# Two attention phases of a transformer kernel: norm, projections and score maxima one batch earlier in a software pipeline

## Chip, cores and metric

One core of a Trainium2 chip runs the whole program. The metric is device time in microseconds from the program's start to its end: the median of three runs is 3821.44 us before the change (3792.84, 3821.44, 3825.76).

## What is computed

Four transformer layers over 16 batches of 256 tokens with 128 channels. Each layer adds a gated attention and a gated feed-forward part to the residual `x`. The change touches the attention of layer 0 (called a0 in the kernel) and an attention with rotary position codes that lies inside layer 2's feed-forward part (a4). Both are causal, with 16 heads of 8 channels; the core of each, per batch, is

```python
q, k, v = to_heads(q), to_heads(k), to_heads(v)      # 16 heads x 8 channels
q = q * gate[None, :, :, None]                       # a0 only; a4 rotates q and k instead
scores = jnp.einsum('bhqd,bhkd->bhqk', q, k) / scale
scores = jnp.where(causal, scores, -jnp.inf)
attn = jax.nn.softmax(scores, axis=-1)
out = jnp.einsum('bhqk,bhkd->bhqd', attn, v)
```

Two other attentions use the same function: a1 (layer 1, 32 heads, differential) and a2 (layer 2, 16 heads, one key head, not causal).

## The kernel before

`attention_phase` is one function for all four attentions. It writes five instruction streams (SP, POOL, ScalarE, TensorE, VectorE) that meet in semaphores: `after(engine, signal, b, k)` waits until the k-th event of batch b has happened. Each stream runs its instructions in the order written.

**Steps and slots.** The work is a software pipeline over the 16 batches. `steps` calls `step(t, m)` for t from -3 to 16: -3 to 0 written out, 1 to 12 as a loop of four turns with three steps in its body (`Fori`), 13 to 16 written out. A step has one slot for each head (16 in a0, a2 and a4). In step t, batch t gets its exponentials and values, batch t+1 its score maxima, batch t+2 its projections, batch t+3 its norm; batch t-1 its output projection. `QH`, `KH`, `VX`, `H` and `CX` have three places for this, indexed modulo 3.

**A batch's way, with slots of a0 and a4.** Norm of t+3: mean (slot 4, a0 only), square, variance (slot 7), `VE`, power on POOL (8), diagonal `DG` (9), its broadcast on TensorE (L680, slot 10), `XN`, `H` (12). Projections of t+2: Q and K at slot 0 in a0 (L656, L657); in a4 Q at slot 0 and K at slot 2 (L653, L654), each with a rotation over VectorE (L804, L805) and POOL. V follows (L662, slot 2 or 4). Then q and k are split into three bf16 parts each (`SPL`), and SP sends the parts to `QH` and `KH` in 64 KB DMAs, first the parts (L436, L437), then, when these have landed, copies of them within `QH` and `KH` (L442, L444). Score maxima of t+1: for each head three matmuls into one of three PSUM banks (L587 to L589), and one reduction on VectorE into `NM3` (L784). The 16 heads are spread over slots 0 to 12, so slots 4, 8 and 12 have two. `scores` waits until at most two of the reductions before it are open, but heads 0, 1 and 2 wait until all of the previous batch's are done.

**The maxima's way back.** The maxima of heads 0 to 7 (group 0) are gathered at slot 8 (L852, L853), transposed into PSUM bank 7 at slot 10 (L728), split into two bf16 rows at slot 11 (L559 on ScalarE, L881 on VectorE); POOL then sends the two rows to `QH` (L485, L487). Group 1 follows at slots 13, 15 and 16, that is slot 0 of the next step. In step t the transposed scores of head p (`scores_t`, L605 to L607) need these rows: heads 0 to 7 from slot 0 on (L605 waits for `m_sent`), heads 8 to 15 from slot 8 on. ScalarE takes the exponential (L549), and every four heads TensorE multiplies with the values (L628).

**Bank 7** is shared by the turns of the context (L635, slots 4 and 12), the output's transposes and matmul (L707, L712, slots 6 and 7) and the maxima's transposes (L728). Each waits for the one before it by a hand-written condition (`turns_before`).

**Lead-in.** Rows of `QH` and `KH` that hold masks are filled once for each ring place (`fill`, L740), four VectorE copies each: place 0 before the steps, places 1 and 2 in slots 5, 8, 9 and 11 of steps -3 and -2.

## Time and profile before

| | us |
|---|---|
| median of three runs | 3821.44 |
| lowest and highest | 3792.84, 3825.76 |
| span of the profiled execution | 3792.6 |
| mean granted TensorE clock, share of full speed | 0.833 |
| a0: first exponential of batch 0 to last of batch 15 | about 83 to 391 |
| a4: the same | about 2290 to 2654 |

The profile is of one execution whose span is about the lowest of the runs. TensorE is busy for 72% of it, VectorE for 60%, ScalarE for 35%, POOL for 29%.

How rows are read. A group of instructions has its source line, engine, operation, output and input by their names, shapes and count; behind the bar the busy time and the mean ns of one, behind the second bar the idle time of the engine just before them and what ended it. A window has start and end, its length, busy time (and count of instructions) of PE (matmuls), PEld (weight loads), DVE (VectorE), ACT (ScalarE) and POOL, then the granted clock (1.00 is the full 2.4 GHz, 0.50 is 1.2 GHz), the share of time in which the DMA engines were busy, and GB/s. A timeline row has start, duration, engine, line and operation, and in brackets the idle time before it and what ended that. Times are us from the start of the span.

### The profile page before, as it was taken

To read this page: it belongs to the slowest core of one execution; us is meant where nothing else is said; L and a number is where in the kernel's file an instruction comes from. 1 tells how busy PE (TensorE), PEld (TensorE's weight loads), DVE (VectorE), ACT (ScalarE), POOL (GpSimd) and SP (SyncE) were. 2 spreads that over 40 slices of the span, in tenths; PEclk is the share of its full clock that TensorE was granted. 3 is DMA by queue.
4 is the path that set the end of the run, shared out by engine and by line. 5 is a ranking of instruction groups with operands and counts; after the bars stand their busy time and mean duration, and the time that the engine had idled before them with its cause. 6 is when DMAs were issued, how large, how long until landed. Compare 5 with 4: busy or idle time off the path is not lost. (4 is left out here: it accounts for less than half of the span.)

```text
span 3792.6 us, 71700 instructions
## 1 busy us (share of the span) xinstructions
PE 2747.7 (72%) x20731; PEld 1822.0 (48%) x20756; DVE 2269.6 (60%) x5526; ACT 1329.9 (35%) x3004; POOL 1103.8 (29%) x1121
## 2 busy tenths in 40 slices
PE   4778624228788887878499966777799964568899
PEld 3555523216566666367255554555544631145344
DVE  4666672148788875322477755555555689965555
ACT  1555201005555553333166623444322221123321
POOL 2222107743333332646322222222100144421000
PEclk6999856558999998889599977888899965579899
DMA  3332302334334321355211102222000000000000
GB/s 70 42 43 35 120 34 56 45 75 60 50 42 53 42 33 50 122 120 101 65 25 24 20 14 36 35 35 27 27 1 0 1 3 0 0 6 23 4 0 22
DMA packets 154624, 148.12 MB, mean 39 GB/s; under 512 B 29433, under 2 KB 135554, under 8 KB 149378
## 3 DMA queue, kind: packets, MB, share of 16 engines
q1 hardware_dynamic: 118882, 121.52, 16.7%
q0 software_dynamic: 34336, 21.83, 4.0%
q8 instruction: 133, 2.18, 0.3%
q10 hardware_dynamic: 1152, 1.61, 0.1%
q14 instruction: 121, 0.99, 0.1%
HBM read 52.70 MB, written 33.01 MB: 23 GB/s over the span
## 5 line engine op out<-in xcount | busy, mean ns | idle before, releaser
L549 ACT ACTIVATE a1PR<-bank 128x384 f32<-128x384 f32 x512 | 242.9, 493 | 152.8 <-PE bank L607 149.3
L784 DVE TENSOR_REDUCE a1NM<-bank 128x3 f32<-128x384 f32 x512 | 263.1, 549 | 30.9 <-PE bank L589 27.9
L784 DVE TENSOR_REDUCE a4NM<-bank 128x3 f32<-128x384 f32 x256 | 132.8, 550 | 140.8 <-PE bank L589 139.0
L787 DVE TENSOR_REDUCE a2NMQ<-bank 128x2 f32<-128x512 f32 x256 | 168.1, 685 | 64.7 <-PE bank L593 64.4
L784 DVE TENSOR_REDUCE a0NM<-bank 128x3 f32<-128x384 f32 x256 | 134.1, 551 | 96.9 <-PE bank L589 95.6
L549 ACT ACTIVATE a4PR<-bank 128x384 f32<-128x384 f32 x256 | 122.2, 490 | 190.5 <-PE bank L607 190.1
L953 PE MATMUL bank<-ONES 128*128 128x256 bf16 x960 | 170.0, 284 | 23.5 <-DMA f3nWR<-in_wr 4.0
L549 ACT ACTIVATE a2PR<-bank 128x512 f32<-128x512 f32 x256 | 149.6, 596 | 99.3 <-PE bank L611 97.2
L1509 POOL TENSOR_TENSOR lM<-lF,lV 128x1024 f32<-128x1024 f32 x32 | 122.2, 3818 | 168.3 <-DVE lF L1522 167.8
L549 ACT ACTIVATE a0PR<-bank 128x384 f32<-128x384 f32 x256 | 121.9, 490 | 136.1 <-PE bank L607 135.6
L605 PE MATMUL bank<-a1QH,a1KH 128*128 128x128 bf16 x512 | 117.2, 230 | 56.1 <-ACT a1PR L549 42.1
L2157 POOL DMA_INDIRECT routed<-yY,yID x80 | 123.6, 1545 | 84.0 <-DMA routed<-yY,yID 39.8
L1374 ACT ACTIVATE f2eSG<-bank 128x512 f32<-128x512 f32 x96 | 57.3, 597 | 193.1 <-PE bank L1321 182.1
L1410 DVE TENSOR_TENSOR f3eT<-f3eSG,bank 128x512 f32<-128x512 f32 x88 | 60.5, 688 | 106.7 <-PE bank L1324 96.4
L587 PE MATMUL bank<-a1KH,a1QH 128*128 128x128 bf16 x512 | 113.3, 227 | 8.9 <-DVE a1NM L784 4.4
L953 PEld LDWEIGHTS bank<-ONES 128*128 128x128 bf16 x960 | 99.5, 118 | 41.1 <-issue 8.4
L1374 ACT ACTIVATE f3eSG<-bank 128x512 f32<-128x512 f32 x88 | 52.6, 597 | 188.9 <-PE bank L1321 188.9
L1410 DVE TENSOR_TENSOR f2eT<-f2eSG,bank 128x512 f32<-128x512 f32 x96 | 66.0, 687 | 87.7 <-PE bank L1324 78.7
L606 PE MATMUL bank<-a1QH,a1KH 65*128 65x128 bf16 x512 | 115.8, 228 | 0.0
L607 PE MATMUL bank<-a1QH,a1KH 128*128 128x128 bf16 x512 | 115.0, 226 | 0.0
L1487 PE MATMUL bank<-CST,lAT 128*128 128x128 f32 x32 | 15.1, 472 | 137.8 <-DVE lAT L1555 137.8
L628 PE MATMUL bank<-a1PR,a1VX 128*32 128x256 f32 (+1 forms) x2048 | 114.3, 342 | 0.0
(676 smaller groups left out, 8668.5 us busy)
## 6 DMA issues: line engine op xcount, KB each, us to landing
yWT<-in_w SPq DMA_DIRECT2D x40, 256.0 KB, 3.2
a1QH<-a1SPL SPq DMA_DIRECT2D x96, 64.0 KB
a1KH<-a1SPL SPq DMA_DIRECT2D x96, 64.0 KB
a1QH<-a1QH SPq DMA_DIRECT2D x96, 64.0 KB
a1KH<-a1KH SPq DMA_DIRECT2D x96, 64.0 KB
rows_by_slot<-gZB SPq DMA_DIRECT2D x5, 1040.0 KB
yXG<-rows_by_slot SPq DMA_DIRECT2D x40, 130.0 KB, 3.2
sums<-rZT SPq DMA_DIRECT2D x2, 2112.0 KB
```

The costliest lines, as they stand in the source:

```text
L549: nc.scalar.activation(PR[:, h % 8, :], bank[2 + h % 2][:, 0:NC], ACT.Exp, scale=SCALE)\
L587: pe.matmul(o[:, 0:P], q(0), k(0), start=True, stop=True)
L605: pe.matmul(o[:, 0:P], k(0), q(0), start=True, stop=True)
L606: pe.matmul(o[:, P:2 * P], k(0, FREE), q(1, FREE), start=True, stop=True)
L607: mm = pe.matmul(o[:, 2 * P:3 * P], k(1), q(1), start=True, stop=True)
L628: mm = pe.matmul(o, w, rhs, start=(a == 0 and n == 0), stop=(a == PK - 1 and n == 1), skip_group_check=True)
L784: v.tensor_reduce(NM3[:, h, :], S_BANK[h % 3][:, 0:NC].rearrange("p (n k) -> p n k", n=3), AX, ALU.max, negate=True).then_inc(s_used.sem, 1)
L787: v.tensor_reduce(NMQ[:, :, h], S_BANK[h % 3][:, 0:NC].rearrange("p (n k) -> p n k", n=2), AX, ALU.max, negate=True).then_inc(s_used.sem, 1)
L953: pe.matmul(bank[7][:, 0:2 * P], spare[:, 0:P], spare[:, :], start=True, stop=True)
L1410: v.tensor_tensor(T1[:, :], a, bank[2 + q][:, :], ALU.mult).then_inc(t1_ready.sem, 1)
L1509: nc.gpsimd.tensor_tensor(M1[:, j, :, :, :], fk, vv, ALU.mult).then_inc(m1.sem, 1)
L2157: nc.gpsimd.indirect_dma_start(ACC[a][:, :], bass.IndirectOffsetOnAxis(ID2[:, j % 4, a:a + 1], 0), Y[:, j % 4, a, :], None, bounds_check=D ...
```

## The change

The number of steps of lead is now a setting, `lead`: 4 for a0 and a4, 3 as before for a1 and a2. With 4, batch t+4 gets its norm in step t, batch t+3 its projections. Score maxima begin at slot 5 two steps ahead (`first_score=-11`): heads 0 to 10 of batch t+2 in slots 5 to 15 of step t, heads 11 to 15 of batch t+1 in slots 0 to 4, one head for each slot. Group 0's maxima are gathered at slot 13 two steps ahead (`nmq=(-3, 8)`), transposed at slot 15, split and sent at slot 0 one step ahead; group 1's at slots 8, 10 and 11 one step ahead. `QH`, `KH`, `VX`, `H` and `CX` get a fourth place, with one more set of fills (step -2). The steps now run from -4 to 16: five written out, a loop of two turns with four steps in its body, eight written out. The conditions of bank 7 are replaced by `bank7_free`, which waits for the previous user in slot order, in all four attentions.

The diff, cut to its core (the rest replaces 3 by `LEAD` in indices in the same way):

```diff
+    LEAD = cfg["lead"]
 
     with ExitStack() as ctx:
         sb = lambda name, shape, dt=F32: c.sb(cfg["name"] + name, shape, dt, ctx)
-        QH = sb("QH", [KROWS, 3, NH, T], BF16)
-        KH = sb("KH", [KROWS, 3, HK, T], BF16)
-        VX = sb("VX", [P, 3, 2 * SV // PK, 2 * PK, 16])
+        QH = sb("QH", [KROWS, LEAD, NH, T], BF16)
+        KH = sb("KH", [KROWS, LEAD, HK, T], BF16)
+        VX = sb("VX", [P, LEAD, 2 * SV // PK, 2 * PK, 16])
...
+        LOOPED = (NB - 1 - LEAD) // LEAD * LEAD
+
         def steps(eng, step):
 
-            for t in range(-3, 1):
-                step(t, t % 3)
-            with eng.Fori(0, 4) as i:
-                for k in range(1, 4):
-                    step(i * 3 + k, k % 3)
-            for t in range(13, 17):
-                step(t, t % 3)
+            for t in range(-LEAD, 1):
+                step(t, t % LEAD)
+            with eng.Fori(0, LOOPED // LEAD) as i:
+                for k in range(1, LEAD + 1):
+                    step(i * LEAD + k, k % LEAD)
+            for t in range(LOOPED + 1, NB + 1):
+                step(t, t % LEAD)
...
-        L_SCORES = 0
-        N_SCORES = cfg["score_slots"]
+        L_SCORES, N_SCORES = cfg["first_score"], cfg["score_slots"]
         heads_at = lambda h: range(*(min(max(k - L_SCORES, 0), N_SCORES) * NH // N_SCORES for k in (h, h + 1)))
-
-        L_NMQ = [16, 28] if diff else [8, 13]
+        scored_at = lambda h: [(a, n) for a in (1, 2) for n in heads_at(h - (a - 1) * NH)]
+
+        L_NMQ = cfg["nmq"]
+        L_MT = [n + 2 for n in L_NMQ]
         L_HALF = [n + 3 for n in L_NMQ]
+        ahead = lambda h, at: [(g, 1 - n // NH) for g, n in enumerate(at) if n % NH == h]
...
-        turns_before = lambda h: sum(p < h for p in turn_at)
...
+        turned_users = [(p % NH, 0, -(p // NH), cx_ready, s + 1) for s, p in enumerate(4 * PK * (s + 1) + 4 for s in range(NS))]
+        bank7_users = sorted(turned_users + [(L_OUT, 1, -1, tmp_ready, 1)]
+                             + [(n % NH, 2, 1 - n // NH, mlo_ready, g + 1) for g, n in enumerate(L_MT)], key=lambda u: u[:2])
+
+        def bank7_free(pe, t, h, order):
+
+            place = [n for n, u in enumerate(bank7_users) if u[:2] < (h, order)]
+            place = place[-1] if place else -1
+            for back in range(len(bank7_users)):
+                slot, kind, offset, signal, k = bank7_users[(place - back) % len(bank7_users)]
+                offset -= place - back < 0
+                if not isinstance(t, int):
+                    after(pe, signal, t + offset, k)
+                    return
+                if 0 <= t + offset < NB:
+                    after(pe, signal, t + offset, k)
...
-                if isinstance(t, int) and -2 <= t <= 0:
+                if isinstance(t, int) and t <= 0 and has(LEAD - 1, t):
                     sp.wait_ge(zeroed, 2)
-                    sp.wait_ge(rows_ready, 4 * (t + 2) + 2)
-                if has(2, t):
-                    b, j = t + 2, (m + 2) % 3
+                    sp.wait_ge(rows_ready, 4 * (t + LEAD - 1) + 2)
+                if has(LEAD - 1, t):
+                    b, j = t + LEAD - 1, (m + LEAD - 1) % LEAD
...
-                        after(sp, st_ready, b - 3)
+                        after(sp, st_ready, b - LEAD)
...
-                    for g in range(2):
-                        back = L_HALF[g] // NH
-                        if h == L_HALF[g] % NH and has(1 - back, t):
-                            after(pool, mlo_ready, t + 1 - back, g + 1)
-                            after(pool, go, t + 1 - back, g)
+                    for g, a in ahead(h, L_HALF):
+                        if has(a, t):
+                            after(pool, mlo_ready, t + a, g + 1)
+                            after(pool, go, t + a, g)
                             nc.gpsimd.tensor_tensor(GO[:, :], c.HALF[0:1, 0:2], c.HALF[0:1, 0:2], ALU.add).then_inc(go.sem, 1)
-                            for a in range(2):
-                                pool.dma_start(QH[MAX0 + a:MAX0 + a + 1, (m + 1 - back) % 3, g * HG:(g + 1) * HG, :], M2[:, g, a, :])\
+                            for n in range(2):
+                                pool.dma_start(QH[MAX0 + n:MAX0 + n + 1, (m + a) % LEAD, g * HG:(g + 1) * HG, :], M2[:, g, n, :])\
...
-                if h == 0 and isinstance(b, int) and b < 2:
-                    pe.wait_ge(rows_ready, 4 + 8 * b)
+                if h == 0 and isinstance(b, int) and b < LEAD:
+                    pe.wait_ge(rows_ready, 4 + 4 * b)
...
-                    if has(1, t):
-                        for n in heads_at(h):
-                            scores(t + 1, (m + 1) % 3, n)
-                    if has(2, t):
-                        b, j = t + 2, (m + 2) % 3
+                    for a, n in scored_at(h):
+                        if has(a, t):
+                            scores(t + a, (m + a) % LEAD, n)
+                    if has(LEAD - 1, t):
+                        b, j = t + LEAD - 1, (m + LEAD - 1) % LEAD
...
-                            after(pe, cx_ready, b, s)
-                            if turns_before(L_OUT) == s and not back:
-                                after(pe, tmp_ready, b - 1)
-                            for g in range(2):
-                                if turns_before(L_NMQ[g] + 2) == s and has(1 - back, t):
-                                    after(pe, mlo_ready, t + 1 - back, g + 1)
+                            bank7_free(pe, t, h, 0)
...
-                    for g in range(2 if has(1, t) else 0):
-                        b = t + 1
-                        if h == L_NMQ[g] + 2:
+                    for g, a in ahead(h, L_MT):
+                        if has(a, t):
+                            b = t + a
                             if causal:
                                 after(pe, nmq_ready, b, 2 * g + 2)
                             else:
                                 after(pe, s_used, b, HG * (g + 1))
-                            if has(0, t):
-                                after(pe, cx_ready, t, turns_before(L_NMQ[g] + 2))
-                            if has(-1, t):
-                                after(pe, tmp_ready, t - 1)
-                            if g:
-                                after(pe, mlo_ready, b, g)
+                            bank7_free(pe, t, h, 2)
...
-                if h == 0 and not causal:
-                    after(v, mt_ready, b - 1)
+                if h % HG == 0 and not causal:
+                    after(v, mt_ready, b - 1, h // HG + 1)
...
-                        for n in heads_at(h):
-                            maxima(b, n)
-                        for g in range(2):
-                            heads = slice(g * HG, (g + 1) * HG)
-                            if h == L_NMQ[g] and causal:
-                                after(v, s_used, b, HG * (g + 1))
-                                after(v, mt_ready, b - 1, g + 1)
-                                v.tensor_copy(NMQ[:, 0, heads], NM3[:, heads, 0]).then_inc(nmq_ready.sem, 1)
-                                v.tensor_tensor(NMQ[:, 1, heads], NM3[:, heads, 1], NM3[:, heads, 2], ALU.min).then_inc(nmq_ready.sem, 1)
+                    for a, n in scored_at(h):
+                        if has(a, t):
+                            maxima(t + a, n)
+                    for g, a in ahead(h, L_NMQ) if causal else ():
+                        if has(a, t):
+                            b, heads = t + a, slice(g * HG, (g + 1) * HG)
+                            after(v, s_used, b, HG * (g + 1))
+                            after(v, mt_ready, b - 1, g + 1)
+                            v.tensor_copy(NMQ[:, 0, heads], NM3[:, heads, 0]).then_inc(nmq_ready.sem, 1)
+                            v.tensor_tensor(NMQ[:, 1, heads], NM3[:, heads, 1], NM3[:, heads, 2], ALU.min).then_inc(nmq_ready.sem, 1)
...
-                            fill(t + 4, (part,))
+                            fill(t + LEAD + 1, (part,))
...
-        attention_phase(c, dict(ln, name="a0", score_slots=13, layer=0, NH=16, HK=16, HV=16, VW=8, CW=128, causal=True,
+        attention_phase(c, dict(ln, name="a0", lead=4, first_score=-11, score_slots=16, nmq=(-3, 8), layer=0, NH=16, HK=16, HV=16, VW=8, CW=128, causal=True,
...
-        attention_phase(c, dict(name="a4", score_slots=13, layer=2, centered=False, eps=rms["neps"], NH=16, HK=16, HV=4, VW=8, CW=128,
+        attention_phase(c, dict(name="a4", lead=4, first_score=-11, score_slots=16, nmq=(-3, 8), layer=2, centered=False, eps=rms["neps"], NH=16, HK=16, HV=4, VW=8, CW=128,
```

## Rows read from the trace of the kernel before

**Rows 1.** Groups by line, a0, eight steps from 185 us.

```profile
L605 PE MATMUL bank<-a0QH,a0KH 128*128 128x128 bf16 x128 | 28.8, 228 | 15.0 <-DMA a0QH<-a0M 15.0
```

**Rows 2.** Groups by line, a4, eight steps from 2412 us.

```profile
L605 PE MATMUL bank<-a4QH,a4KH 128*128 128x128 bf16 x128 | 29.6, 234 | 29.9 <-DMA a4QH<-a4M 29.9
```

**Rows 3.** Windows: eight steps of a0, eight of a4, two of a2.

```profile
185.00:344.00 159.00, 126.10 (x1520) 93.97 (x1521) 105.38 (x280) 88.03 (x208) 44.52 (x72) 0.94 0.32 41
2412.00:2604.00 192.00, 139.98 (x1536) 101.76 (x1536) 105.94 (x288) 84.28 (x208) 55.74 (x88) 0.86 0.26 34
1967.40:2005.00 37.60, 34.03 (x321) 21.47 (x322) 29.29 (x64) 25.24 (x52) 11.12 (x18) 1.00 0.15 24
```

**Rows 4.** Timeline of an a4 step boundary: last DMAs, then TensorE's first matmuls.

```profile
2478.00 1.12 POOL L487 DMA_DIRECT2D a4QH<-a4M  x2 [0.25 <-issue]
...
2479.37 1.28 SPq L444 DMA_DIRECT2D a4KH<-a4KH  x1
...
2483.63 0.29 PE L605 MATMUL bank<-a4QH,a4KH 128*128 128x128 bf16 x1 [3.56 <-DMA a4QH<-a4M]
...
2484.36 0.29 PE L587 MATMUL bank<-a4KH,a4QH 128*128 128x128 bf16 x1 [0.23 <-DMA a4KH<-a4KH]
```

**Rows 5.** Timeline of slots 0 to 5 of the a4 step before.

```profile
2460.52 1.17 PE L653 MATMUL bank<-a4H,a4WQ 128*128 128x256 f32 x2
...
2465.10 0.65 PE L653 MATMUL bank<-a4H,a4WK 128*128 128x256 f32 x2
...
2467.00 1.96 DVE L784 TENSOR_REDUCE a4NM<-bank 128x3 f32<-128x384 f32 x4
...
2468.03 0.22 PE L587 MATMUL bank<-a4KH,a4QH 128*128 128x128 bf16 x1
2468.66 0.55 SPq L435 DMA_DIRECT2D a4QH<-a4ZR  x1
```

**Rows 6.** Timeline of TensorE in a4: starts of steps 0 and 13 to 15.

```profile
2289.93 0.27 PE L605 MATMUL bank<-a4QH,a4KH 128*128 128x128 bf16 x1 [4.62 <-DMA a4QH<-a4M]
...
2604.09 0.27 PE L605 MATMUL bank<-a4QH,a4KH 128*128 128x128 bf16 x1 [3.82 <-DMA a4QH<-a4M]
...
2604.68 1.17 PE L653 MATMUL bank<-a4H,a4WQ 128*128 128x256 f32 x2
...
2624.50 0.22 PE L605 MATMUL bank<-a4QH,a4KH 128*128 128x128 bf16 x1 [2.58 <-DMA a4QH<-a4M]
...
2628.62 0.26 PE L587 MATMUL bank<-a4KH,a4QH 128*128 128x128 bf16 x1 [3.78 <-DMA a4KH<-a4KH]
...
2643.18 0.23 PE L605 MATMUL bank<-a4QH,a4KH 128*128 128x128 bf16 x1 [0.19 <-ACT a4PR L549]
```

**Rows 7.** Timeline of a0: starts of steps 0, 13 to 15, last exponentials.

```profile
82.47 0.29 PE L605 MATMUL bank<-a0QH,a0KH 128*128 128x128 bf16 x1 [4.78 <-DMA a0QH<-a0M]
...
344.02 0.22 PE L605 MATMUL bank<-a0QH,a0KH 128*128 128x128 bf16 x1 [1.45 <-DMA a0QH<-a0M]
...
362.23 0.22 PE L605 MATMUL bank<-a0QH,a0KH 128*128 128x128 bf16 x1 [3.73 <-DMA a0QH<-a0M]
...
379.80 0.22 PE L605 MATMUL bank<-a0QH,a0KH 128*128 128x128 bf16 x1 [1.60 <-DMA a0QH<-a0M]
...
389.68 0.87 ACT L549 ACTIVATE a0PR<-bank 128x384 f32<-128x384 f32 x2 [0.58 <-PE bank L607]
```

**Rows 8.** Lead-in: first score maxima (timeline), then the fills (window of L740).

```profile
64.61 0.29 PE L587 MATMUL bank<-a0KH,a0QH 128*128 128x128 bf16 x1 [7.36 <-DMA a0KH<-a0KH]
...
2268.66 0.27 PE L587 MATMUL bank<-a4KH,a4QH 128*128 128x128 bf16 x1 [9.53 <-issue]
...
49.00:61.00 12.00, 5.06 (x4) 0.50 0.46 55
```

**Rows 9.** a1: timeline at one loop turn, and one turn's window.

```profile
1018.99 0.28 PE L605 MATMUL bank<-a1QH,a1KH 128*128 128x128 bf16 x1 [3.58 <-issue]
...
1019.00:1131.20 112.20, 91.25 (x1110) 67.58 (x1110) 90.00 (x252) 64.94 (x153) 39.61 (x36) 0.94 0.34 46
```

More of the change, by code:

```diff
@@ L457, in step @@
                 for h in range(NH):
-                    if has(3, t):
-                        b = t + 3
+                    if has(LEAD, t):
+                        b = t + LEAD
                         if h == L_VE:
@@ L510, in step @@
                 for h in range(NH):
-                    if has(3, t):
-                        b = t + 3
+                    if has(LEAD, t):
+                        b = t + LEAD
                         if h == L_SQ:
@@ L552, in step @@
                         copy_set(t - copy_at[h][1], copy_at[h][0])
-                    for g in range(2):
-                        back = L_HALF[g] // NH
-                        if h == L_HALF[g] % NH and has(1 - back, t):
-                            b = t + 1 - back
+                    for g, a in ahead(h, L_HALF):
+                        if has(a, t):
+                            b = t + a
                             after(act, mt_ready, b, g + 1)
@@ L876, in step @@
                             v.tensor_tensor(DST[:, tok(b)], DST[:, tok(b)], TMP[:, :], ALU.add).then_inc(x_updated.sem, 1)
-                    for g in range(2):
-                        back = L_HALF[g] // NH
-                        if h == L_HALF[g] % NH and has(1 - back, t):
-                            after(v, mhi_ready, t + 1 - back, g + 1)
+                    for g, a in ahead(h, L_HALF):
+                        if has(a, t):
+                            after(v, mhi_ready, t + a, g + 1)
                             v.tensor_tensor(M2[:, g, 1, :], bank[7][0:HG, 0:T], M2[:, g, 0, :], ALU.subtract).then_inc(mlo_ready.sem, 1)
```

62 lines of the change are left out of this document (30 added, 32 removed).

## The prediction

> **What bounds the kernel now.** I read four views, in this order. First the two groups of line 605 (the first transposed-score matmul of each head) in eight consecutive steps of the first attention (a0) and of the fourth (a4): TensorE stood idle 15.0 us before it in a0 and 29.9 us in a4, and the releaser named is the DMA that writes the maxima rows of `QH` [rows 1, 2]. That is 1.88 and 3.74 us a step, always at head 0.
>
> Next, the windows over the same eight steps: 159 us in a0, 192 us in a4, so 19.9 and 24.0 us a step, with a granted clock of 0.94 and 0.86 [rows 3]. The third row there is two steps of the third attention (a2), which has nearly the same slots: clock 1.00, TensorE busy 34.0 of 37.6 us. Without a stall at the step's head this pipeline can therefore run almost solidly on TensorE, at full clock.
>
> Then the timeline of one a4 boundary. POOL issues the two row writes of group 0 (L487) at 2478.00, and TensorE, which is through with slot 15, stands still for 3.56 us until 2483.63 [rows 4]. Meanwhile SP is issuing the last of its 64 KB copies of the next batch's `KH` (2479.37), and `KH` itself holds the next matmul up to 2484.36. So the maxima rows are asked for 5 slots after they are sent, and land behind large copies. Last, the clock: the fp32 pair of L653 takes 1.17 us right after the stall [rows 5], and the same pair 0.65 us some 5 us later at full clock; the stall is paid a second time as half clock.
>
> **The change, part by part.**
>
> *Maxima rows one pipeline step earlier.* Group 0's rows are now sent at slot 0 of the step before the one that reads them, 16 slots ahead instead of 5; group 1's at slot 11, 13 slots ahead instead of 8. Sixteen slots are a whole step, over 16 us, against 5.6 us from issue to use in [rows 4]. The wait goes: 1.88 and 3.74 us a step.
>
> *The clock.* A clock of 0.94 means 12% of 159 us at the lower level, 2.4 us a step. TensorE is working in nearly all of it, and half of it comes back: 1.2 us. In a4 0.86 gives 6.7 us a step, of which I put 1.9 (half of the stall) where TensorE idles anyway; half of the other 4.8 is 2.4 us. Why it should stay up: without the stall a0 has 2.2 us of idle time a step left (159 - 126.1 - 15.0, over eight), and a2 holds 1.00 with 1.8 [rows 3].
>
> *What is late next.* Slots 8 and 12 lose one of their two heads of maxima, which covered waits for `DG` and `M2`. One head is three matmuls at about 0.06 us, so I add 0.3 us a step for two such places. The other new wait: maxima of batch b+1, head 0 (slot 5) need all 16 of batch b's to be used, the last of which is issued one slot earlier; before, the step's end lay between. In a4 VectorE works off four reductions from 2467.00 to 2468.96, where TensorE comes to slot 5's maxima at 2468.03 [rows 5]. One of those four disappears (slot 4 now has one head), and slot 5's own comes after, so the needed one ends at about 2467.98: a cost between nothing and 0.75 us (a reduction and its signal). I take nothing and keep 18 us (24 steps) for the range.
>
> *The copies.* From the Q projection (2460.52) to the landing of the last `KH` copy (2484.36) are 23.8 us [rows 4, 5], and again from 2604.68 to 2628.62, where the lighter step made TensorE wait 3.78 us for it [rows 6]. Before, a step of 24.0 just covered that. Now there is a step and five slots: 18.2 + 5.7 = 23.9 us, while about 2.5 us of the chain (projections at half clock) should go. It fits with some 2.5 us to spare. SP's own queue issues for 12 of each 18 us.
>
> *Sum of one full step.* a0: 19.9 - 1.88 - 1.2 + 0.3 = 17.1 us. a4: 24.0 - 3.74 - 2.4 + 0.3 = 18.2 us. VectorE is then busy for 13.2 of them in either, 77% and 73%, below its 78% in a2 and its 80% in a1, where no step is held up by it for long [rows 3, 9].
>
> *Whole phases, from batch 0's first exponential.* Norm work now ends after step 11, projections after 12, and step 14 holds 5 heads of maxima instead of 16. a0 before: 82.47 to 390.55, 308.1 us [rows 7]. After: 12 x 17.1 = 205.2; steps 12 and 13 are the old 13 and 14, 35.8 less stalls of 3.73 and 1.60 and 1.2 of clock, 29.3; step 14 lies 5/16 of the way from a bare last step (10.75) to a step with maxima (14.6), 12.0; the last one 10.75. Together 257.2: a gain of 50.9 us. a4 before: 2289.93 to 2643.18 and a last step as in a0, 364.0 us [rows 6]. After: 12 x 18.2 = 218.4; the old 13 and 14, 39.1 less 2.58, 3.78, 0.19 and 2.4, 30.1; 12.1; 10.75. Together 271.4: a gain of 92.6 us.
>
> *The fifth lead-in step.* Batch 0's copies still land when they did: TensorE stood for 7.36 us in a0 and 9.53 us in a4 before the first maxima [rows 8], and batch 1's projection now moves into that hole. But between its first maxima and its first exponential lay 21.3 us in a4 (17.9 in a0), and now lie 11 heads with the fourth ring place's fills among them (11 x 0.49 + 5.1 for four copies [rows 8] + about 2 of norm work on VectorE, 12.5 us) and another step of maxima without exponentials, as long as the old one less the stall at its end, 17.9 - 4.78 = 13.1 (a4: 21.3 - 4.62 = 16.7) [rows 6, 7]. That is 25.6 and 29.2 us: a loss of 8 in each, 16 us in all. The larger clearing of `VX` on POOL lies under VectorE's first fills.
>
> *The loop.* The body grows from three steps to four and turns once instead of three times. In the second attention (a1) TensorE loses 3.58 us at each turn with no releaser but "issue"; its body has 1110 matmuls [rows 9]. a0's has 190 matmuls a step (1520 in eight [rows 3]), 570 in all, and turns with none but the DMA waits above. The new bodies have 760, nearer to 570, so I take nothing; the other end is two turns of 3.58 and the half clock behind them, 10 us.
> The Trainium skill (Runtime: NRT & Kernel Launch, Instruction fetch mechanics) says that a taken branch to a target outside the prefetched window must fetch it first, and gives TensorE room for 2048 instructions; with one weight load for each matmul a1's 2220 exceed that, and 1520 do not, register instructions apart. By that rule, too, the turn costs nothing; by a1's row it would cost 10 us.
>
> *Second and third attention.* They keep three places; only the waits ahead of bank 7 are written differently, for the same last user. Nothing, with 10 us either way (0.3 us in each of their 32 steps).
>
> Net: 50.9 + 92.6 - 16 = 127.5 us. The profiled execution spans 3792.6 us, about the lowest of the three runs; the median is 3821.4. I subtract from the median: **3694 us**; the profiled span should be near 3665.
>
> **The rivals.** *The copies take the wait's place* (14%). If denser steps make the 23.8 us grow to 27, TensorE waits about 1.5 us at slot 5 in each a4 step and the clock falls again: 12 x (1.5 + 2.4) = 47 us given back, 3741. For: the 3.78 us of [rows 6]. Against: five more slots of slack, and projections at full clock.
> *The clock stays as it is* (13%). The 2.2 us of idle time left in each step may be enough to hold it down. Then 12 x (1.2 + 2.4) = 43 us are lost, 3737. Against: a2's 1.00 [rows 3].
> *SP's copies set the period* (3%), the case on the other side. SP serves the batches in order, and from first issue (2468.66) to last landing are 15.7 us. Should that stretch to the old step length at the denser pace, the steps stay at 19.9 and 24.0, only the wait's name changes, and the lead-in's 16 us remain: 3837, slower by 0.4%. It decides from 18.2 us on, and is over 1% slower only from about 25 us a step on.
> *A smaller gain by the loop turns and the slot-5 handshake together* (8%): 28 us less, 3722.
> The forecast itself has 62%.
>
> **How the numbers follow.** The forecast and the three dearer variants with a gain span 3694 to 3741, and the other attentions add 10 on top; with the median's 29 us above the profiled run as play, I set the upper end at 3755. Lower end: 0.3 us a step kept (7), the other attentions' 10 and a median as near the lowest run as the profile is: 3645. Faster by over 1% (below 3783) are all cases but the SP one, less a little for causes I don't see: 0.92; within 1%, which is about what a measurement of this kernel can tell from no change, 0.06; slower 0.02.
>
> **What the next profile would show.** Right: no DMA wait at line 605 in a0 and a4; clocks near 1.0; steps of 17 and 18 us; about 8 us more before the first exponential. Wrong: an idle time before line 587 at slot 5, by `KH` (copies) or by VectorE's reduction (handshake); a clock still under 0.9; an "issue" gap of 3.6 us in the middle of each phase.

## The result, and the profile after

| | before | after |
|---|---|---|
| median, us | 3807.14 | 3670.71 |
| lowest and highest (four runs each) | 3790.24, 3825.76 | 3662.05, 3685.97 |
| span of the profiled execution | 3792.6 | 3666.1 |
| a0, first instruction to last | 369.5 | 334.0 |
| a0, of that before the first exponential | 55.9 | 65.4 |
| a4, first instruction to last | 429.4 | 339.8 |
| a4, of that before the first exponential | 59.9 | 66.0 |
| a1, a2 | 656.9, 347.8 | 650.9, 348.1 |

The changed kernel takes 0.9671 of the time before (95% interval 0.963 to 0.9713). The forecast was 3694 us, with a span near 3665. A phase's length here and below is read from the first and last timeline row that names a tile of the phase, a step's from its first transposed-score instruction to the next step's. Of the 126.5 us of span, a4 gave 89.6, a0 35.5, a1 6.0, and 4.6 went back in a2 and in front of and between the phases.

Lines have moved: what was L605 is L624 (first transposed-score matmul), L587 is L606 (first matmul of a head's maxima), L680 is L699, L635 is L654, L549 is L569, L740 is L748. From here on a turn is the jump from the end of a loop's body back to its start: a loop that runs its body four times has three turns, the new loops of a0 and a4 have one each.

Windows of the kernel after, eight steps of a0 (4 to 11) and eight of a4 (4 to 11); columns as in [rows 3]:

```profile
168.60:306.70 138.10, 117.92 (x1522) 90.02 (x1520) 105.80 (x281) 85.52 (x209) 44.22 (x72) 0.99 0.36 50
2329.80:2473.10 143.30, 122.56 (x1536) 92.86 (x1535) 106.17 (x289) 83.66 (x208) 55.61 (x88) 0.99 0.34 48
```

Against [rows 3]: 17.3 us a step instead of 19.9, 17.9 instead of 24.0, with TensorE doing the same 1520 and 1536 matmuls. The clock is 0.99 instead of 0.94 and 0.86, so the same matmuls also count for less busy time (117.9 against 126.1, 122.6 against 140.0).

The same two stretches, groups by line on TensorE, first a0's, then a4's:

```profile
L624 PE MATMUL bank<-a0QH,a0KH 128*128 128x128 bf16 x128 | 28.6, 223 | 6.7 <-issue 3.4 <-ACT a0PR L569 3.2
L654 PE MATMUL bank<-CST,a0CTS 128*128 128x128 f32 x32 | 6.5, 286 | 6.5 <-DVE a0M L887 6.5
L699 PE MATMUL bank<-a0DG,ONES 128*128 128x128 f32 x32 | 5.7, 300 | 6.4 <-DVE a0DG L845 6.4
...
L624 PE MATMUL bank<-a4QH,a4KH 128*128 128x128 bf16 x128 | 28.5, 223 | 3.8 <-issue 3.8
```

The DMA wait of [rows 1, 2] is gone from both: in a4 nothing is left of its 29.9 us. What stands before L624 now is one stop of 3.4 and one of 3.8 us without a releaser, and in a0 four short waits for ScalarE (3.2 us together). The timeline shows the two stops at the heads of steps 5, where the new loop turns:

```profile
188.91 0.28 PE L624 MATMUL bank<-a0QH,a0KH 128*128 128x128 bf16 x1 [3.35 <-issue]
...
2351.18 0.23 PE L624 MATMUL bank<-a4QH,a4KH 128*128 128x128 bf16 x1 [3.76 <-issue]
```

They are the shape of a1's turn in [rows 9]. And a wait that the prediction did not have: in the waits of ScalarE over a0, the first split of a batch's queries (L556) waits for the DMAs of the batch before, because `SPL` has one place. The signal that it waits for (`parts_sent`) counts more than the reads of `SPL`: it holds the landing of the last parts, of two rows of zeros and of the six copies within `QH` and `KH`, which don't read `SPL`, and the releaser named is one of these copies. The columns are what waited, for what, the sum in us, how often, and the longest:

```profile
ACT a0SPL L556 <- DMA a0KH<-a0KH: 23.8, 12, 6.5
```

Its two longest are in the lead-in and in step 0 (timeline, ScalarE, then TensorE; ahead of the second, SP's last issue that reads `SPL` and its last copy):

```profile
68.83 0.62 ACT L556 CAST a0SPL<-a0QKF 128x512 bf16<-128x512 f32 x1 [6.54 <-DMA a0KH<-a0KH]
...
91.78 0.61 SPq L458 DMA_DIRECT2D a0KH<-a0SPL  x1
...
98.16 1.35 SPq L465 DMA_DIRECT2D a0KH<-a0KH  x1
...
103.19 0.62 ACT L556 CAST a0SPL<-a0QKF 128x512 bf16<-128x512 f32 x1 [5.92 <-DMA a0KH<-a0KH]
...
104.26 0.29 PE L624 MATMUL bank<-a0QH,a0KH 128*128 128x128 bf16 x1 [5.78 <-ACT a0PR L569]
```

The last read of `SPL` was issued 6.4 us before the last copy, so the place may have been free well before the split was let go. The exponentials of step 0 stand behind the split in ScalarE's order, and TensorE's next scores wait 5.78 us for a bank that they free. That step took 23.3 us; the eleven behind it average 17.1. (How much of step 0 the one place of `SPL` costs is taken up again with the experiments: in two other kernels with one place it took 19.3 and 19.5.)

### The profile page after: what moved, and what is told of

Its sections match the earlier page's. It is cut to its first block and busy times, and to the rows that moved or that the text cites. A ratio compares the mean times of both kernels' runs of the same rounds, so it can differ in the third digit from the quotient of the medians.

```text
span 3666.1 us, 70823 instructions
## 1 busy us (share of the span) xinstructions
PE 2720.9 (74%) x20756; PEld 1809.7 (49%) x20756; DVE 2283.8 (62%) x5534; ACT 1324.2 (36%) x3004; POOL 1106.0 (30%) x1121
## 3 DMA queue, kind: packets, MB, share of 16 engines
q1 hardware_dynamic: 118882, 121.52, 17.1%
## 5 line engine op out<-in xcount | busy, mean ns | idle before, releaser
L569 ACT ACTIVATE a1PR<-bank 128x384 f32<-128x384 f32 x512 | 242.4, 492 | 149.0 <-PE bank L626 145.8
L569 ACT ACTIVATE a2PR<-bank 128x512 f32<-128x512 f32 x256 | 149.7, 596 | 96.4 <-PE bank L630 94.3
L624 PE MATMUL bank<-a1QH,a1KH 128*128 128x128 bf16 x512 | 116.0, 228 | 57.0 <-ACT a1PR L569 42.2
L569 ACT ACTIVATE a4PR<-bank 128x384 f32<-128x384 f32 x256 | 121.2, 489 | 93.9 <-PE bank L626 93.0
L569 ACT ACTIVATE a0PR<-bank 128x384 f32<-128x384 f32 x256 | 120.2, 489 | 81.3 <-PE bank L626 80.3
L606 PE MATMUL bank<-a1KH,a1QH 128*128 128x128 bf16 x512 | 113.7, 227 | 5.1 <-DVE a1NM L792 3.3
L2218 ACT ACTIVATE yHS<-bank,yFB 128x256 f32<-128x256 f32 x160 | 66.0, 470 | 135.2 <-PE bank L2176 135.2
L607 PE MATMUL bank<-a1KH,a1QH 65*128 65x128 bf16 x512 | 114.8, 230 | 0.0
L608 PE MATMUL bank<-a1KH,a1QH 128*128 128x128 bf16 x512 | 114.7, 230 | 0.0
```

Of the source, the lines that this page charges most:

```text
L569: nc.scalar.activation(PR[:, h % 8, :], bank[2 + h % 2][:, 0:NC], ACT.Exp, scale=SCALE)\
L606: pe.matmul(o[:, 0:P], q(0), k(0), start=True, stop=True)
L607: pe.matmul(o[:, P:2 * P], q(1, FREE), k(0, FREE), start=True, stop=True)
L608: mm = pe.matmul(o[:, 2 * P:3 * P], q(1), k(1), start=True, stop=True)
L624: pe.matmul(o[:, 0:P], k(0), q(0), start=True, stop=True)
```

## The experiments

Each kernel is the changed one with the edit shown, unless it says otherwise. Ratios are to runs of the kernel before made beside them: median 3793.18 us (19 runs) for the kernels with late maxima, three steps of lead, two places of `SPL` alone and no loop in a0 and a4; 3797.03 (11 runs) for all others but the one with six steps in the body, which has a single run of 3794.76 beside it. Where only one run of a kernel was made, the text says so.

### Maxima as late as before, all else as changed

In the calls of a0 and a4:

```diff
-lead=4, first_score=-11, score_slots=16, nmq=(-3, 8)
+lead=4, first_score=0, score_slots=13, nmq=(8, 13)
```

> Four ring places, norm and projections one step earlier as in the change, but the maxima where they were before: 16 heads in slots 0 to 12 one step ahead, the maxima rows sent at slots 11 and 16. Theory (the whole gain comes from sending the maxima rows earlier, through the wait and the half clock behind it): the DMA wait before line 624 at each step's head is back with 1.5 to 4 us, the steps are 19 to 20 us in a0 and 22 to 24 us in a4, and with the longer lead-in the time is that of the kernel before within 1%, 3780 to 3830 us. Rival (the fourth place alone, by taking the KH copies off the step's head, gives a good part): steps of a4 under 21 us and a time under 3740 us.

Measured: 3774.22 us, 0.9944 of before (0.9914 to 0.9973), so 19 of some 125 us are left. That is 6 us below the 3780 that was expected at the least, a4 having gained at its end (below). a0 took 375.8 us and a4 412.8. Windows of eight steps of a0 and of a4, and the groups of L624 over the same stretches:

```profile
178.30:339.10 160.80, 126.39 (x1520) 94.95 (x1520) 104.63 (x280) 88.13 (x208) 44.23 (x72) 0.93 0.31 43
2386.70:2576.50 189.80, 139.21 (x1537) 102.78 (x1538) 105.96 (x288) 84.38 (x208) 55.48 (x88) 0.86 0.26 35
```

```profile
L624 PE MATMUL bank<-a0QH,a0KH 128*128 128x128 bf16 x128 | 28.9, 228 | 19.1 <-DMA a0QH<-a0M 15.0 <-issue 4.0
L624 PE MATMUL bank<-a4QH,a4KH 128*128 128x128 bf16 x129 | 29.8, 234 | 37.8 <-DMA a4QH<-a4M 37.8
```

What follows: the fourth place and the earlier norm and projections by themselves bring back neither the wait nor the clock: 15.0 us in eight a0 steps is the figure of [rows 1], and the clocks 0.93 and 0.86 are about those of [rows 3] (0.94 and 0.86). The steps are 20.1 and 23.7 us. The gain in the steps is the maxima's time. What a4 did gain here (429.4 to 412.8, in spite of a longer lead-in) came in its last steps: the waits for `KH` of [rows 6] are not there, and steps 13 and 14 took 14.3 and 13.2 us.

### Three steps of lead: only the waits ahead of bank 7 differ

In the calls of a0 and a4:

```diff
-lead=4, first_score=-11, score_slots=16, nmq=(-3, 8)
+lead=3, first_score=0, score_slots=13, nmq=(8, 13)
```

> The changed kernel with all four attentions at three places and the old slots, so only the rewritten waits of bank 7 differ from the kernel before. Theory: nothing, ratio 1.000 within 0.3%, and the second attention takes what it took before, 657 us within 2. Rival (the rewritten waits account for the 6 us that the second attention lost in the changed kernel's profile): second attention at 651 us within 2.

Measured: 3784.51 us, 0.9974 (0.9932 to 1.0017). No difference is clear of the noise, though the interval reaches down to 26 us of gain. The phases: a0 363.6, a1 646.5, a2 347.4, a4 427.1 us. a1 is below both numbers that had been named for it (657 and 651, within 2), and a0 lies 5.9 and 7.4 us under its two profiles of the kernel before. With one profile of this kernel, whether a few us of that come from the rewritten waits isn't shown. It doesn't touch the maxima's part: the kernel with late maxima has the rewritten waits too, and took 375.8 and 412.8 us where the changed one took 334.0 and 339.8.

### The kernel before, once more

> The kernel before once more, for a second profile of it. All theories: a0 369 us and a4 429 us as in the first profile, within 3. The second attention lay at 657 us in the one profile of before, at 651 in the changed kernel's and at 647 to 659 in those of the variants: if the rewritten waits made a difference it is at 657 again, within 1.5; if it is only the place of the code or chance it may lie anywhere from 646 to 660.

Measured: 3794.57 us in its one run; a0 371.0, a1 654.9, a2 343.9, a4 426.2. So a phase that nobody touched moves by 1.5 to 4 us from one profile to the next. Over the ten profiles whose a1 has its loop, a1 took 644.1 to 662.1 us. The 6.0 us that a1 seemed to gain are inside that, and are not the change's to claim. a0's lead-in moves as well: 57.9 us here, where the first profile had 55.9, and from its first maxima to the first exponential's scores 19.4 instead of 17.9.

### The wait put back at full earliness

The maxima keep their new time, but at head 1 TensorE also waits for the rows of the next batch, which POOL has just sent.

```diff
                 if p % HG == 0:
                     after(pe, m_sent[p // HG], b)
+                if p == 1 and LEAD == 4 and (not isinstance(b, int) or b + 1 < NB):
+                    after(pe, m_sent[0], b + 1)
```

> The changed kernel with one more wait on TensorE in each step of a0 and a4: ahead of head 1's transposed scores it waits for the next batch's group 0 maxima rows, which POOL sends in the same slot, so a DMA wait like the removed one is put back by hand at slot 1. Theory (an idle stretch of 3 us or more is paid again as half clock behind it): a wait of 2.5 to 5 us at line 626, the granted clock in these phases back to 0.85 to 0.93, and steps longer by the wait and a further 1 to 2.5 us. Rival (the lower clock before came from something else in the old slots): steps longer by just the wait, clock 0.97 or more.

Measured: 3792.75 us in its one run; a0 386.9, a4 423.1. Windows of six steps of each, behind the turn, and their groups of L626:

```profile
223.40:345.70 122.30, 95.78 (x1142) 73.50 (x1142) 79.50 (x211) 64.90 (x157) 33.09 (x54) 0.92 0.30 42
2447.90:2583.60 135.70, 102.07 (x1154) 76.00 (x1153) 80.14 (x217) 62.98 (x156) 41.63 (x66) 0.90 0.27 36
```

```profile
L626 PE MATMUL bank<-a0QH,a0KH 128*128 128x128 bf16 x96 | 22.7, 236 | 17.3 <-DMA a0QH<-a0M 17.3
L626 PE MATMUL bank<-a4QH,a4KH 128*128 128x128 bf16 x96 | 22.4, 234 | 23.4 <-DMA a4QH<-a4M 23.4
```

What follows: this is the price of a stall by itself. In a0 the wait is 2.9 us a step (17.3 over six) and the step is 20.4 instead of 16.8 (the eight steps after, less the turn): 3.6 us, 0.7 more than the wait. In a4 it is 3.9 us, and the step 22.6 instead of 17.4: 5.2, 1.3 more than the wait. The clock fell from 0.99 to 0.92 and 0.90. a4's surcharge is in the range that was expected (1 to 2.5 us), a0's is below it. One stall a step was enough to take the clock down, and the surcharge is put down to that clock. The work around the stall is the changed kernel's, so the fall isn't a matter of where the maxima lie.

### Two places for the split parts

ScalarE's split of a batch now waits for the copies of the batch before the last, and SP waits for the last batch's copies before it sends the next.

```diff
-        SPL = sb("SPL", [P, R, 3, 2, T], BF16)
+        NSP = 2 if LEAD % 2 == 0 else 1
+        SPL = sb("SPL", [P, NSP, R, 3, 2, T], BF16)
...
-        after(act, parts_sent[r], b - 1)
+        after(act, parts_sent[r], b - NSP)
...
+        if NSP > 1:
+            after(sp, parts_sent[r], b - 1)
```

> The changed kernel with two places for the bf16 parts of q and k (SPL) in a0 and a4: ScalarE's first split waits for the copies of the batch before the last, and SP waits for the last batch's copies instead. Theory (the new bound in a0 is the round from one split to the next through SP's copies, 16.4 us at least): ScalarE's waits of 0.5 to 6.5 us before the split are gone, TensorE's 5.8 us in a0's step 0 and 3.3 us in the lead-in too; a0 shorter by 8 to 14 us, a4 by 3 to 8, the whole by 0.3 to 0.6% against the changed kernel (ratio to before 0.961 to 0.965). Rival (TensorE's own work is the bound and the waits have slack behind them): less than 3 us in each.

Measured: 3648.02 us, 0.963 of before (0.9604 to 0.9657), where the changed kernel has 0.9671. The intervals overlap a little. a0 took 327.4 us instead of 334.0, with a lead-in of 62.9 (65.4) and a step 0 of 19.9 us (23.3); a4 did not move (339.9). So the ratio came out as expected and the phases did not: 8 to 14 us were expected of a0 and 3 to 8 of a4. Of the 21.0 us by which this profile's span is shorter than the changed kernel's, a0 has 6.6; a1 has 3.9, a2 6.2 and what lies around the phases the rest, all code that the edit leaves alone. What the second place is shown to give is a0's 6.6 us, and 7.1 between the two kernels without a loop further down (325.1 and 318.0). The three written-out a0 steps behind the loop, as a window:

```profile
249.20:295.50 46.30, 42.45 (x573) 33.14 (x571) 38.88 (x106) 32.11 (x78) 16.42 (x27) 1.00 0.40 51
```

15.4 us a step, with TensorE busy for 14.2 of them; the changed kernel took 16.0, 16.7 and 17.0 in the same three. The one place of `SPL`, with the wide signal that guards it, was a bound of a0: ScalarE's waits fell from 23.8 to 3.2 us. A signal for the reads of `SPL` alone is the obvious rival to a second place, and was not tried. Steps 9 to 11 gained 3.3 us together, but steps 12 to 15 gave back 2.5, for in step 13 TensorE now waits longer for the landing of `KH` itself (1.37 us in the changed kernel). In a4 that wait had been there already (3.05), and stayed:

```profile
316.27 0.22 PE L609 MATMUL bank<-a0KH,a0QH 128*128 128x128 bf16 x1 [3.27 <-DMA a0KH<-a0KH]
...
2472.88 0.22 PE L609 MATMUL bank<-a4KH,a4QH 128*128 128x128 bf16 x1 [3.18 <-DMA a4KH<-a4KH]
```

### a0 and a4 without a loop

```diff
-        LOOPED = (NB - 1 - LEAD) // LEAD * LEAD
+        LOOPED = 0 if LEAD == 4 else (NB - 1 - LEAD) // LEAD * LEAD
...
```

> The changed kernel with all 21 steps of a0 and a4 written out, no loop. Theory (the gap of 3.4 and 3.8 us with no releaser but issue at step 5, and the slower step behind it, belong to the loop's turn): both gaps gone, steps 4 and 5 as long as the others (16.5 and 17.4 us), 3.5 to 5 us less in each of a0 and a4, 7 to 10 us in all. Rival (longer straight code costs as much in fetches as the turn did): the same gap of over 1 us appears at some other places, and the sum of the steps stays within 2 us.

Measured: 3653.91 us, 0.9639 (0.9623 to 0.9655); a0 325.1 us, a4 329.1. Windows of eight a0 steps and ten a4 steps:

```profile
162.00:295.00 133.00, 115.70 (x1520) 88.61 (x1518) 105.22 (x280) 85.05 (x209) 43.88 (x72) 1.00 0.38 51
2291.00:2458.00 167.00, 149.42 (x1927) 115.03 (x1924) 132.19 (x361) 105.12 (x262) 69.10 (x110) 1.00 0.38 51
```

16.6 and 16.7 us a step, at a clock of 1.00. a0 and a4 together are 19.6 us shorter than in the changed kernel, where 7 to 10 were expected. No stop of over 1 us without a releaser is left in them from batch 0's first scores on, but one of 1.34 us in a4's step 1. a4's two steps around the turn take 21.2 and 19.0 us in the changed kernel, 5.4 more than two of their neighbours of 17.4: the stop of 3.76 and the clock behind it. Here they take 16.6 each. But the other steps inside a4's loop shrank too, from 17.4 or 17.5 to 16.6. They hold the same work; the changed kernel itself takes 16.6 in two of the three full steps behind its loop, and 17.5 in the other. So a loop costs here beyond its turns, and which part of that is the waits on computed values isn't told apart by these runs.

The price turned up elsewhere as well. a1, whose code is the same in both kernels, took 659.5 us here (650.9), and two of its three turns in the timeline are these (after, then this kernel):

```profile
989.02 0.28 PE L624 MATMUL bank<-a1QH,a1KH 128*128 128x128 bf16 x1 [3.78 <-issue]
...
1101.71 0.29 PE L624 MATMUL bank<-a1QH,a1KH 128*128 128x128 bf16 x1 [3.82 <-issue]
```

```profile
979.46 0.29 PE L625 MATMUL bank<-a1QH,a1KH 128*128 128x128 bf16 x1 [7.23 <-issue]
...
1092.94 0.29 PE L625 MATMUL bank<-a1QH,a1KH 128*128 128x128 bf16 x1 [6.95 <-issue]
```

The third turns are 3.59 and 7.33. The same turn costs twice as much with only the code ahead of it changed. What it is about that code wasn't tried. Some more of it needn't do it: a0 is written with 11 copies of a step's code in the kernel before, 14 in the one with six steps in the body (below) and 17 in the changed one, and a1's turns take 3.4 to 3.9 us in all three; here there are 21.

### The kernel before with six steps in a loop's body

```diff
-            with eng.Fori(0, 4) as i:
-                for k in range(1, 4):
-                    step(i * 3 + k, k % 3)
+            BODY = 3 if diff else 6
+            with eng.Fori(0, 12 // BODY) as i:
+                for k in range(1, BODY + 1):
+                    step(i * BODY + k, k % 3)
```

> The kernel before with one size changed: in a0, a2 and a4 the loop's body has six steps instead of three and turns once instead of three times (between steps 6 and 7). Nothing else differs. The before's bodies hold 1337 (a0) and 1145 (a4) TensorE instructions with matmuls, weight loads and register instructions, and its turns show no idle time but the DMA wait. The new ones hold about 2670 and 2290. Theory (a turn's price hangs on the size of the body): an idle time of 3 to 4 us marked issue at the head of step 7, in the place of the DMA wait or beside it, fetches in the instruction queue during the whole loop, and no more at the heads of steps 4 and 10 than the DMA wait. Phase a0 then 369 to 373 us, since the idle time partly takes the wait's place. Rival (the changed kernel's turns are dear for its new waits in front of bank 7, not for the size): the head of step 7 shows the DMA wait of about 1.9 us (a0) and 3.7 us (a4) as its neighbours do, no issue, and no fetches in the instruction queue between step 2 and step 11.

Measured: 3799.31 us in its one run; a0 372.6, a2 348.6, a4 431.3. The new turn lies at the head of step 7. In a2, where the maxima's wait is small, it stands clear beside its neighbour at step 6 (the kernel before has 0.34 us, by the DMA, at this same place, where its short body turns too); in a0 it is in the DMA wait's place:

```profile
2005.75 0.28 PE L611 MATMUL bank<-a2QH,a2KH 65*128 65x256 bf16 x1 [0.34 <-DMA a2QH<-a2M]
...
2027.80 0.39 PE L611 MATMUL bank<-a2QH,a2KH 65*128 65x256 bf16 x1 [3.90 <-issue]
...
206.45 0.23 PE L606 MATMUL bank<-a0QH,a0KH 128*128 128x128 bf16 x1 [1.80 <-DMA a0QH<-a0M]
228.67 0.29 PE L606 MATMUL bank<-a0QH,a0KH 128*128 128x128 bf16 x1 [3.79 <-DMA a0QH<-a0M]
```

In a4 the DMA wait is about as long as the stop and hides most of it: 4.38 us at the turn, 3.70 and 3.56 at the heads beside it.

Instructions are fetched over DMA queues of their own, of which q8 is the larger. The DMA queues in 190 to 344 us (in the kernel before and in this one inside a0's loop, in the changed kernel its loop's second run, to 257 us, and the written-out steps behind it), with packets, MB and share of the engines, first of the kernel before, then of the kernel after, then of this one:

```profile
q1 hardware_dynamic: 7776, 6.42, 32.1%
q0 software_dynamic: 960, 0.13, 0.8%
```

```profile
q1 hardware_dynamic: 7808, 6.43, 31.0%
q8 instruction: 15, 0.25, 0.7%
```

```profile
q1 hardware_dynamic: 7737, 6.16, 30.3%
q8 instruction: 15, 0.25, 0.7%
```

What follows: the changed kernel's waits aren't in this one, and the stop of 3.8 to 3.9 us is. With three steps in the body nothing is fetched in the loop; with six, code is fetched all through, and with the changed kernel's four too (7 of its 15 packets fall in the loop). The theory of the body's size holds, and the rival that blamed the new waits falls. The queue doesn't name the engine that fetches, and a second one, q14, goes the same way (no packets before, 7 and 13 in the other two); that the size that counts is TensorE's is taken from the stop, which is TensorE's own. One thing was short of what was expected: a0's turn is still put down to the DMA, only 2.0 us longer than its neighbour. And one number in the text of what was expected belongs elsewhere: 1145 instructions, and 2290 for the doubled body, are a2's; a4's are 1349 and 2696.

### The fourth place's fills one step earlier

```diff
-                    for part in range(4 if isinstance(t, int) and t < -1 else 0):
+                    for part in range(4 if isinstance(t, int) and t < min(-1, 2 - LEAD) else 0):
                         if h == L_FILL[part]:
                             fill(t + LEAD + 1, (part,))
+                        if t == -3 and LEAD == 4 and h == L_XN + 1 + part:
+                            fill(3, (part,))
```

> The changed kernel with the fourth place's fills in slots 12 to 15 of step -3 instead of among the first maxima in step -2. Theory (the fills, 5 us on VectorE, lie on the lead-in's path where they are now): first exponential 3 to 5 us sooner after the phase's start in a0 (65.4 us in the changed kernel's profile) and a4 (66.0). Rival (TensorE's lead-in is bound by the copies of batches 0 and 1, so the fills are hidden): less than 1 us.

Measured: 3673.28 us in its one run; the lead-ins are 65.4 and 65.7 us, as in the changed kernel (65.4, 66.0). The changed kernel has the fills of 1.22 to 1.69 us each between 71.95 and 81.51 us, among the first maxima. Moving them brought nothing to the lead-in as a whole: the way from first maxima to the first exponential's scores is 0.7 us shorter in a0 and 2.2 in a4, and the first maxima come about as much later. In the lead-in ScalarE's split stood waiting for the copies in this kernel too, to within 0.01 us as long; in step 0 TensorE's wait behind the split was shorter than the 5.78 us of the changed kernel, and the step took 19.3 us:

```profile
69.03 0.62 ACT L556 CAST a0SPL<-a0QKF 128x512 bf16<-128x512 f32 x1 [6.55 <-DMA a0KH<-a0KH]
...
102.97 0.23 PE L624 MATMUL bank<-a0QH,a0KH 128*128 128x128 bf16 x1 [2.42 <-ACT a0PR L569]
```

### Two places for the split parts, and no loop in a0, a1 and a4

The two edits together, the second with `LOOPED = 0 if LEAD == 4 or diff else ...` (`diff` is true for a1 alone).

> Two places for SPL in a0 and a4 and all steps of a0, a1 and a4 written out, in one kernel. Theory (the copies' round and the loops are two separate bounds, and each hides a part of the other's gain in a0: with one place and no loop its steps are 16.4 to 16.7 us, with two places but in the loop 16.2, with two places and behind the loop 15.5): a0's steps 15.5 us, a4's 16.6, a1 shorter by its three turns (3.4 us each and the slower clock behind them) and by 0.5 us or more in each of twelve steps, 15 to 25 us; 3600 to 3620 us in all. Rival (the gains overlap, or straight code in a1 is held up by fetches): over 3630 us, with gaps of the releaser issue inside a1's steps.

Measured: 3616.15 us, 0.9527 of before (0.949 to 0.9563). That is the fastest kernel of this study, 1.5% under the changed one. a0 318.0 us, a1 626.9, a2 341.9, a4 326.2. Windows of seven a0 steps and nine a4 steps:

```profile
173.60:284.90 111.30, 99.74 (x1332) 77.52 (x1331) 90.94 (x246) 74.93 (x182) 38.28 (x63) 1.00 0.40 54
2264.20:2414.20 150.00, 134.22 (x1733) 103.34 (x1729) 118.90 (x325) 94.50 (x235) 62.13 (x99) 1.00 0.38 51
```

15.9 and 16.7 us a step, where 15.5 and 16.6 were expected. a1 is 17 us under the shortest of its looped profiles, so there the gain is more than play: three turns went, with the clock behind them, and no stop of over 1 us without a releaser is left where its loop was. a0 is bounded anew by its copies: at 306.61 us TensorE waits 2.74 us for `KH`.

## Why the prediction was right, step by step

**The wait and its clock: right, in size too.** The prediction took 1.88 + 1.2 us out of an a0 step and 3.74 + 2.4 out of an a4 step. Less the turn, eight steps of after take (138.1 - 3.4) / 8 = 16.8 and (143.3 - 3.8) / 8 = 17.4 us, so 3.1 and 6.6 went. That is 3.1 forecast for a0, and 6.1 for a4. The late-maxima kernel shows that all of it hangs on the rows' time, and the kernel with the wait put back shows that the clock falls with the stall: a surcharge of 0.7 and 1.3 us there, for waits of 2.9 and 3.9 us. Those surcharges are smaller than the 1.2 and 2.9 us that before and after differ by beyond the wait itself; that stall also stood elsewhere in the step's work, at head 1 instead of head 0, and what share of the difference this makes isn't shown.

**The 0.3 us for `DG` and `M2`: wrong.** Each of the two waits moved, the sum didn't. Before, L635 and L680 waited for these two:

```profile
L635 PE MATMUL bank<-CST,a0CTS 128*128 128x128 f32 x32 | 6.5, 286 | 5.4 <-DVE a0M L881 5.4
L680 PE MATMUL bank<-a0DG,ONES 128*128 128x128 f32 x32 | 5.7, 300 | 8.6 <-DVE a0DG L837 8.6
```

14.0 us in eight steps, against 6.5 + 6.4 = 12.9 after: 0.1 us a step less, not 0.3 more. In a4 it is 5.4 + 7.6 = 13.0 against 6.5 + 4.6 = 11.1, 0.2 less. A likely reason, which no run isolates: the head of maxima that covered the wait for `DG` had also occupied VectorE, which makes `DG`, so that with the cover the thing waited for came sooner as well. The term looked at one side only.

**The loop's turn: the term that was mis-sized.** It was taken as 0, with two turns of 3.58 us and the clock behind them, 10 us, as the other end. The other end was right: 3.35 and 3.76 us of stop, and with the clock behind them about 4 us in a0 (20.1 + 17.5 less two steps of 16.8) and 5.4 in a4. The reason given was that 760 matmuls are nearer to 570 than to 1110. But the size that decides lies somewhere between them: counted over one turn in the trace, with weight loads and register instructions, TensorE's body before holds 1337 instructions in a0, some 1145 in a2 and 1349 in a4, and the turns of a0 and a2 are free (a4's can't be told from its DMA wait, but nothing is fetched in its loop either); 1762 (a0) and 1778 (a4) after, and a1's 2591, cost 3.4 to 3.8 us. Six steps in the old body give 2672 in a0 and some 2290 in a2, and a2's turn then costs 3.9 us. The traces bracket the limit (free at 1337, dear at 1762); nearness to one of two ends was no argument where no row lay between. The Trainium skill (Runtime: NRT & Kernel Launch, Instruction fetch mechanics) gives TensorE room for 2048 instructions. By that figure a body of 1762 fits, yet its turn costs what a1's does: here the measurement decides.

**The copies: right for a4, and a bound missed in a0.** The prediction weighed the chain from projection to `KH` (23.8 us) and found 2.5 us to spare. In a4 that held: L606 waits 0.6 us once in the eight steps. What it did not look at is how soon the next batch may begin. `SPL` has one place, and a batch's first split waits until all copies of the one before have landed. This is the third rival's mechanism, SP's copies setting the period, in small. It put the rival at 3% because 15.7 us of copies is less than 18.2 of step; for the 16.2 to 17 of an a0 step, with the issue and the split on top, it no longer is. It cost 2.5 us of a0's lead-in (the second place of `SPL` took them away) and about a microsecond in each step behind the loop, 16.0 to 17.0 against 15.4, of which step 13 gives most back. What it cost step 0 is less clear: 23.3 us in the changed kernel, 19.9 with the second place, but also 19.3 and 19.5 with one place in the kernels with moved fills and without a loop. So why step 0 lies 6.2 us above the forecast stays open. The rows that would have told of the bound are [rows 4, 5] themselves, though they are a4's: 15.7 us from first issue to last landing, beside a forecast step of 17.1, leaves 1.4 us for all that lies between two batches, as long as the split waits for the copies too.

**The lead-in: right.** The stretch from first maxima to the first exponential's scores was put at 25.6 us in a0 and 29.2 in a4. After, it is 24.4 and 27.9 (L606 from 70.78 to L624 at 95.14, and from 2231.42 to 2259.35), against 17.9 and 21.3 before. That is 6.5 and 6.6 us of the 8 taken for each. The table has 9.5 and 6.1 for the lead-in as a whole, 7.5 for a0 if the second profile of the kernel before is taken. a0's further 3 us lie ahead of its first maxima, which come 40.7 us after the phase's start (37.5 before); there the split waits for the copies, and with the second place of `SPL` it is 38.7. The working put 5.1 us on the fills; moving them took only 0.7 and 2.2 us out of this stretch and nothing out of the lead-in. That term was mis-sized although its sum was near.

**The slot-5 handshake: right at nothing.** In neither of the two stretches does L606 wait for VectorE.

**The sum.** From batch 0's first scores to its last exponential, as the prediction counted, a0 took 263.5 us where 257.2 were forecast: step 0 took 6.2 more, and steps 1 to 11 together 188.6 against 188.1. a4 took 269.3 where 271.4 were forecast: steps 0 to 11 214.0 against 218.4, the last four 55.3 against 53.0, with a wait of some 3 us for `KH` at step 13. So the gain was 44.6 - 9.5 + 94.9 - 6.1 = 123.9 us against 127.5. Some of the match is luck: the two turns' 9.5 us, not counted, and step 0's 6.2 stand against 0.3 us a step put in too much, a4's larger return of clock and a cheaper lead-in. The span came within 1.1 us of the 3665 forecast. The median, 3670.71, is 23 us below the 3694, because the forecast was taken off a median of 3821.44 that three runs had given: with four it is 3807.14, and later sets of 19 and 11 runs gave 3793.18 and 3797.03.

**Bank 7's waits: right at nothing**, within what a1's own play of 18 us and an interval of -26 to +6 us for the kernel with three steps of lead allow one to say.

## What to carry to other kernels

In this pipeline a short stall at the same place of every step was paid twice, once as idle time and once as lower clock (2.9 us cost 3.6, 3.9 cost 5.2), so data that cross a DMA queue full of large copies are worth asking for a whole step ahead. When a stall is taken out, look next at every buffer with a single place: what its round takes, from first write to the signal that sets it free, can be the new floor of the step, as `SPL`'s was in a0, even where the data themselves arrive in time; and see whether that signal waits for more than the last read. And count TensorE's instructions in a loop's body before making it longer: here a turn was free at 1337 and cost 3.4 us or more from 1762 on, and writing the steps out gave some 0.3% of the whole in two phases (the intervals overlap a little) and, with a1's and a second place for the split parts, 1.5%.

## What the runs showed of the hardware that was not expected

- A loop's turn can cost 3.4 to 3.9 us of TensorE, and the very same loop (a1's) 7.0 to 7.3 us in a kernel in which only the code ahead of it differs.
- Steps inside a4's loop took 17.4 us where the same steps written out took 16.6, at a clock of 0.99 and 1.00.
- A body of 2672 instructions of TensorE is fetched all through the loop (15 fetches, 0.25 MB in 154 us), and in a0, a2 and a4 no stop near 1 us without a releaser comes of it but at the turn; one of 1337 isn't fetched again at all.
